# Local attention over a turn of four tiles: another order of steps in the four engine tables

## What is computed

```python
x = attn_layer(shift_tokens(x), Wqkv[i], q_scale[i], k_scale[i], Wo[i]) + x
x = ffn_layer(shift_tokens(x), ln_g[i], ln_b[i], W1[i], b1[i], W2[i], b2[i]) + x
# attn_layer: q, k, v = split(x @ Wqkv), 16 heads of 64
q = l2norm(q) * qs;  k = l2norm(k) * ksc          # then rotary embedding on both
sim = einsum('bhwie,bhwje->bhwij', bq, bk2) * 8   # windows of 32 see themselves and the one before
out = einsum('bhwij,bhwje->bhwie', softmax(masked sim), bv2) @ Wo
# ffn_layer: layernorm, then a * gelu(gate) @ W2
```

## Time and profile before

| | before |
|---|---|
| median of 3 runs | 2223.51 us (2223.18 to 2225.08) |
| profiled execution, whole time | 2226.05 us |
| its span, first to last instruction | 2224.2 us |
| busy in the span: PE, DVE, ACT, POOL | 88%, 66%, 63%, 63% |
| mean granted TensorE clock in the span | 0.909 |
| 24 `back` steps, first to last | 228.0 to 1794.3 us |

### The profile page before, as it was taken

How to read it: one execution, slowest core, us unless ns; L and a number is a source line. 1 busy time by engine, 2 the same in 40 slices (tenths; PEclk the granted TensorE clock), 3 DMA queues, 4 the chain that set the end, 5 groups by cost and what they waited for, 6 DMA issues and landing times. The chain is left out here.

```text
span 2224.2 us, 76642 instructions
## 1 busy us (share of the span) xinstructions
PE 1968.2 (88%) x31783; PEld 1328.2 (60%) x31783; DVE 1461.0 (66%) x2646; ACT 1401.0 (63%) x2766; POOL 1411.5 (63%) x1800
## 2 busy tenths in 40 slices
PE   5659999999999999999999999999999967887293
PEld 4526666666666666666666666666666645554262
DVE  2367777777778778787776877777877635333421
ACT  1167787677776777777777777777777722332041
POOL 1167888778887788887788877888778610001302
PEclk9779999999999999999999999999999966555596
DMA  2011111112110021101201112111101100001311
GB/s 90 0 25 38 61 45 29 38 29 75 32 38 29 29 82 32 31 28 38 76 29 31 29 38 76 28 31 32 34 29 29 31 7 0 1 0 32 99 40 47
DMA packets 55114, 82.88 MB, mean 37 GB/s; under 512 B 13140, under 2 KB 40042, under 8 KB 54002
## 3 DMA queue, kind: packets, MB, share of 16 engines
q1 hardware_dynamic: 53746, 75.88, 11.5%
q0 software_dynamic: 1024, 2.10, 0.3%
HBM read 25.66 MB, written 5.11 MB: 14 GB/s over the span
## 5 line engine op out<-in xcount | busy, mean ns | idle before, releaser
L1068 PE MATMUL b_bank_proj<-layer_weights,b_stream_t 128*128 128x512 f32 x1152 | 588.5, 612 | 34.2 <-DVE b_plain_moved L942 18.1
L942 DVE TENSOR_TENSOR b_plain_moved<-b_bank_proj,b_rope 128x1024 f32<-128x1024 f32 x384 | 463.9, 1219 | 189.0 <-ACT b_squares L828 137.1
L753 POOL TENSOR_TENSOR b_rotated<-b_plain_moved 128x1024 f32<-128x1024 f32 x192 | 453.8, 2363 | 23.6 <-DVE b_plain_moved L942 18.6
L768 POOL TENSOR_TENSOR b_rotated<-b_rotated,b_inv_norm 128x1024 f32<-128x1024 f32 x192 | 365.3, 1903 | 15.6
L859 ACT ACTIVATE b_k_t<-b_bank_shared 64x512 f32<-64x512 f32 x384 | 226.5, 590 | 125.9 <-PE b_bank_shared L1076 123.5
L828 ACT ACTIVATE b_squares<-b_bank_proj 128x512 f32<-128x512 f32 x384 | 229.3, 597 | 115.6 <-PE b_bank_proj L1068 111.2
L1068 PEld LDWEIGHTS b_bank_proj<-layer_weights,b_stream_t 128*128 128x128 f32 x1152 | 186.1, 191 | 135.9 <-issue 44.9
L773 POOL TENSOR_TENSOR b_probs<-b_probs,b_inv_sum 128x512 f32<-128x512 f32 x192 | 200.5, 1045 | 87.2 <-DVE b_inv_sum L963 85.8
L1076 PE MATMUL b_bank_shared<-const_tables,b_rotated 128*128 128x128 f32 x1536 | 233.2, 277 | 22.0 <-POOL b_rotated L768 21.9
L850 ACT ACTIVATE b_q_t<-b_bank_shared 64x512 f32<-64x512 f32 x384 | 225.6, 588 | 34.3 <-PE b_bank_shared L1076 31.5
L1076 PEld LDWEIGHTS b_bank_shared<-const_tables,b_rotated 128*128 128x128 f32 x1536 | 178.1, 141 | 113.4 <-issue 99.2
(11 more groups left out here) (319 smaller groups left out, 2929.1 us busy)
## 6 DMA issues: line engine op xcount, KB each, us to landing
b_v_shifted<-b_v SPq DMA_DIRECT2D x96, 384.0 KB, 3.5
layer_weights<-L_ffn_Wqkv SPq DMA_DIRECT2D x6, 1536.0 KB
b_v_shifted<-b_v SPq DMA_DIRECT2D x72, 128.0 KB, 3.4
d_w<-L_ffn_w SPq DMA_DIRECT2D x16, 256.0 KB, 5.6
layer_weights<-L_ffn_Wo SPq DMA_DIRECT2D x6, 512.0 KB
layer_weights<-L_ffn_W SPq DMA_DIRECT2D x6, 341.0 KB
sorted_rows<-d_zero SPq DMA_DIRECT2D x1, 1472.0 KB, 7.6
expert_rows<-d_sorted_out SPq DMA_DIRECT2D x23, 64.0 KB, 1.5
```

What stands on the lines that cost most here:

```text
L753: nc.gpsimd.tensor_tensor(out=turned[:, k, :], in0=pm[:, k, 0, :], in1=pm[:, k, 1, :], op=ALU.add).then_inc(add_done, 1)
L768: nc.gpsimd.tensor_tensor(out=tk, in0=tk, in1=repeat_last(rn[:, k, :], DH), op=ALU.mult).then_inc(rope_done, 1)
L942: nc.vector.tensor_tensor(to, src.to_broadcast(shape), tab.to_broadcast(shape), ALU.mult).then_inc(mul_done, 1)
L1068: nc.tensor.matmul(out, xs[:, b, t * P:(t + 1) * P], w, start=True, stop=True).then_inc(proj_full, 1)
```

## The change

Only the four lists change. Each holds the same steps as before, so every instruction is still there; their order, and with it the pipelining, differs. What the prediction speaks of, cut from the diff:

```diff
 POOL_TURN
-    ("add", -2, 1), ("clamp", -2, 1), ("weigh", -4, 1), ("rstd", -2, 0), ("rope", -2, 1), ("clamp", -1, 0),
-    ("weigh", -3, 0), ("add", -1, 0), ("weigh", -3, 1), ("clamp", -1, 1), ("rope", -1, 0), ("add", -1, 1),
-    ("rope", -1, 1), ("clamp", 0, 0), ("weigh", -2, 0), ("add", 0, 0), ("rope", 0, 0), ("weigh", -2, 1),
...
+    ("add", -1, 0), ("clamp", -1, 0), ("weigh", -3, 0), ("add", -1, 1), ("clamp", -1, 1), ("weigh", -3, 1),
+    ("rope", -1, 0), ("clamp", 0, 0), ("rope", -1, 1), ("weigh", -2, 0), ("add", 0, 0), ("weigh", -2, 1),
...
+    ("clamp", 2, 0), ("add", 2, 0), ("weigh", 0, 0), ("rope", 2, 0), ("clamp", 2, 1), ("weigh", 0, 1),
+    ("add", 2, 1), ("rope", 2, 1), ("rstd", -1, 0),
 DVE_TURN
-    ("norms", 5, 1), ("residual", 2, 0), ("soft", 4, 0), ("mul", 6, 0), ("norms", 6, 0), ("mul", 6, 1),
-    ("share", 4, 0), ("mul", 6, 2), ("soft", 4, 1), ("residual", 3, 0), ("mul", 6, 3), ("norms", 6, 1),
-    ("share", 4, 1), ("stats", 0, 0), ("soft", 5, 0), ("mul", 7, 0), ("norms", 7, 0), ("share", 5, 0),
+    ("share", 3, 1), ("down", -1, 0), ("mul", 5, 2), ("mul", 5, 3), ("norms", 5, 1), ("residual", 2, 0),
+    ("soft", 4, 0), ("mul", 6, 0), ("mul", 6, 1), ("norms", 6, 0), ("soft", 4, 1), ("share", 4, 0), ("mul", 6, 2),
+    ("residual", 3, 0), ("mul", 6, 3), ("norms", 6, 1), ("share", 4, 1), ("soft", 5, 0), ("mul", 7, 0),
 PE_TURN
-    ("project", 2, 1), ("pv", -1, 0), ("heads_t", 1, 0), ("project", 2, 2), ("heads_t", 1, 1), ("scores", 0, 1),
...
-    ("heads_t", 2, 0), ("project", 3, 1), ("probs_t", 0, 1), ("scores", 1, 1), ("project", 3, 2), ("pv", 0, 0),
-    ("heads_t", 2, 1), ("norm_t", -1, 0), ("project", 3, 3), ("heads_t", 2, 2), ("up", -1, 0), ("heads_t", 2, 3),
-    ("out", 0, 0), ("up", -1, 1), ("enter", 1, 0), ("probs_t", 1, 0), ("scores", 2, 0), ("up", -1, 2),
-    ("up", -1, 3), ("project", 3, 4), ("probs_t", 1, 1), ("project", 3, 5), ("heads_t", 3, 0), ("project", 4, 0),
-    ("project", 4, 1), ("pv", 1, 0), ("heads_t", 3, 1), ("project", 4, 2), ("scores", 2, 1), ("out", 1, 0),
...
+    ("scores", 0, 1), ("leave", -2, 0), ("heads_t", 1, 1), ("project", 2, 3), ("out", -1, 0), ("heads_t", 1, 2),
+    ("heads_t", 1, 3), ("project", 2, 4), ("back", -1, 0), ("probs_t", 0, 0), ("project", 2, 5), ("scores", 1, 0),
+    ("project", 3, 0), ("heads_t", 2, 0), ("project", 3, 1), ("probs_t", 0, 1), ("scores", 1, 1),
+    ("project", 3, 2), ("heads_t", 2, 1), ("pv", 0, 0), ("heads_t", 2, 2), ("heads_t", 2, 3), ("project", 3, 3),
+    ("norm_t", -1, 0), ("out", 0, 0), ("enter", 1, 0), ("up", -1, 0), ("scores", 2, 0), ("probs_t", 1, 0),
+    ("up", -1, 1), ("up", -1, 2), ("up", -1, 3), ("project", 3, 4), ("probs_t", 1, 1), ("project", 3, 5),
+    ("project", 4, 0), ("heads_t", 3, 0), ("project", 4, 1), ("heads_t", 3, 1), ("pv", 1, 0), ("scores", 2, 1),
+    ("project", 4, 2), ("out", 1, 0), ("heads_t", 3, 2), ("heads_t", 3, 3), ("up", -1, 4), ("up", -1, 5),
+    ("probs_t", 2, 0), ("scores", 3, 0), ("project", 4, 3), ("scores", 3, 1), ("probs_t", 2, 1),
 ACT_TURN
-    ("probs_t", -1, 0), ("probs_t", -1, 1), ("project", 2, 0), ("project", 2, 1), ("root", 1, 1), ("exp", 0, 0),
...
-    ("heads_t", 2, 3), ("gelu", -1, 0), ("probs_t", 1, 0), ("gelu", -1, 1), ("enter", 1, 0), ("gelu", -1, 2),
+    ("probs_t", -1, 1), ("project", 2, 0), ("exp", 0, 0), ("root", 1, 1), ("project", 2, 1), ("attended", -1, 0),
...
+    ("attended", 0, 1), ("project", 3, 3), ("heads_t", 2, 2), ("heads_t", 2, 3), ("root", 3, 0), ("gelu", -1, 0),
+    ("gelu", -1, 1), ("gelu", -1, 2), ("enter", 1, 0), ("root", 3, 1), ("project", 3, 4), ("project", 3, 5),
```

More of the change, by code:

```diff
@@ L498 @@
[L498 to L500 removed]
+    ("project", 0, 4), ("project", 0, 5), ("heads_t", 0, 0), ("heads_t", 0, 1), ("project", 1, 0),
+    ("project", 1, 1), ("pv", -2, 0), ("down", -2, 0), ("project", 1, 2), ("project", 1, 3), ("probs_t", -1, 0),
@@ L514 @@
[L514 to L518, removed]
+    ("root", 1, 0), ("probs_t", -1, 0), ("heads_t", 0, 3), ("project", 1, 4), ("project", 1, 5),
@@ new lines @@
+    ("probs_t", -1, 1), ("project", 2, 0), ("exp", 0, 0), ("root", 1, 1), ("project", 2, 1), ("attended", -1, 0),
+    ("heads_t", 1, 0), ("attended", -1, 1), ("project", 2, 2), ("root", 2, 0), ("leave", -2, 0), ("project", 2, 3),
+    ("exp", 0, 1), ("heads_t", 1, 1), ("heads_t", 1, 2), ("heads_t", 1, 3), ("project", 2, 4), ("project", 2, 5),
+    ("root", 2, 1), ("back", -1, 0), ("project", 3, 0), ("heads_t", 2, 0), ("project", 3, 1), ("probs_t", 0, 0),
+    ("probs_t", 0, 1), ("exp", 1, 0), ("project", 3, 2), ("heads_t", 2, 1), ("exp", 1, 1), ("attended", 0, 0),
@@ L519 @@
+    ("project", 4, 4), ("project", 4, 5), ("exp", 3, 1), ("heads_t", 4, 0), ("root", 4, 1), ("project", 5, 0),
+    ("project", 5, 1), ("heads_t", 4, 1), ("attended", 2, 0), ("project", 5, 2), ("attended", 2, 1),
+    ("project", 5, 3), ("heads_t", 4, 2),
 ]
 DVE_TURN = [
-    ("residual", 0, 0), ("hidden", -1, 0), ("mul", 4, 0), ("norms", 4, 0), ("share", 2, 0), ("mul", 4, 1),
-    ("mul", 4, 2), ("soft", 2, 1), ("hidden", -1, 1), ("hidden", -1, 2), ("residual", 1, 0), ("share", 2, 1),
-    ("mul", 4, 3), ("norms", 4, 1), ("soft", 3, 0), ("soft", 3, 1), ("share", 3, 0), ("mul", 5, 0),
@@ L531 @@
-    ("soft", 6, 0),
+    ("residual", 0, 0), ("mul", 4, 0), ("norms", 4, 0), ("mul", 4, 1), ("share", 2, 0), ("soft", 2, 1),
+    ("mul", 4, 2), ("share", 2, 1), ("residual", 1, 0), ("hidden", -1, 1), ("hidden", -1, 2), ("soft", 3, 0),
+    ("mul", 4, 3), ("soft", 3, 1), ("norms", 4, 1), ("share", 3, 0), ("mul", 5, 0), ("mul", 5, 1), ("norms", 5, 0),
+    ("share", 3, 1), ("down", -1, 0), ("mul", 5, 2), ("mul", 5, 3), ("norms", 5, 1), ("residual", 2, 0),
+    ("soft", 4, 0), ("mul", 6, 0), ("mul", 6, 1), ("norms", 6, 0), ("soft", 4, 1), ("share", 4, 0), ("mul", 6, 2),
@@ L532 @@
+    ("residual", 3, 0), ("mul", 6, 3), ("norms", 6, 1), ("share", 4, 1), ("soft", 5, 0), ("mul", 7, 0),
+    ("stats", 0, 0), ("norms", 7, 0), ("soft", 5, 1), ("mul", 7, 1), ("mul", 7, 2), ("share", 5, 0),
+    ("scale", 0, 0), ("mul", 7, 3), ("norms", 7, 1), ("share", 5, 1), ("hidden", 0, 0), ("soft", 6, 0),
 ]
 POOL_TURN = [
-    ("add", -2, 1), ("clamp", -2, 1), ("weigh", -4, 1), ("rstd", -2, 0), ("rope", -2, 1), ("clamp", -1, 0),
-    ("weigh", -3, 0), ("add", -1, 0), ("weigh", -3, 1), ("clamp", -1, 1), ("rope", -1, 0), ("add", -1, 1),
@@ L542 @@
+    ("rope", 0, 0), ("clamp", 0, 1), ("add", 0, 1), ("weigh", -1, 0), ("rope", 0, 1), ("clamp", 1, 0),
+    ("weigh", -1, 1), ("add", 1, 0), ("rope", 1, 0), ("clamp", 1, 1), ("add", 1, 1), ("rope", 1, 1),
+    ("clamp", 2, 0), ("add", 2, 0), ("weigh", 0, 0), ("rope", 2, 0), ("clamp", 2, 1), ("weigh", 0, 1),
+    ("add", 2, 1), ("rope", 2, 1), ("rstd", -1, 0),
 ]
```

22 lines of the change are left out of this document (5 added, 17 removed).

## The result

The changed kernel takes 2247.34 us (median of 4 runs, 2242.76 to 2250.38) against 2223.35 us of the kernel before on the same chip: 1.0106 times, with a 95% interval of 1.0083 to 1.0128. It is 1.1% slower, and above the range of the prediction. Its profiled execution took 2250.05 us, with a span of 2248.2, so 24.0 us more than before.

What follows compares the result with a forecast made beforehand. PE's own list was taken as the bound. From the profiled 2226.05 us, less 15 (layer starts), 0 (ordinary turns), plus 22 (clock), gave 2233, and 2.5 less on the median's scale 2230 us; range 2204 to 2241.

Steps and rivals of the forecast that it cites:

- PE's list: PE's work in an ordinary turn without waits: 65.1 us before the change, 65.0 after.
- The wait before norm_t: With rstd behind rope(2,1), the wait of heads_t(2,2) goes and PE waits 1.9 us before norm_t, bounds 1.2 to 2.1.
- The run saved: 11 runs of products on parts of the array for 12: 0.15 us saved a turn, bounds 0 to 0.19.
- Layer starts: A layer's first turn costs 1.0 us extra for 4.05: 3.0 us won, five times, 15 us; bounds 8 to 19.
- The clock: The wait before norm_t drops PE's clock to half in 14 of 23 turns, about 1.6 us each: 22 us lost.
- The feed of instructions: pv(1) and scores(2,1) as one run ask for 384 instructions in 3.03 us: 0.4 us a turn, bounds 0 to 1.
- Rival 2: Layer starts gain less, or feeding pv(1) with scores(2,1) costs 1 us a turn, no clock loss: 2222 us, no change; chance 0.14.
- The sign: Whole kernel against the one before: faster 0.37, same 0.20, slower 0.43; faster is below 2219 us, slower above 2228.
- rival 1: The wait before norm_t stays too short to cost the clock; only the layers' 15 us remain: 2208 us, faster; chance 0.34.
- The ordinary turn: Turns other than a layer's first: 67.45 us against 67.3 before, nothing won or lost; bounds 66.7 to 68.2.
- Rival 3: POOL becomes the bound, waiting at clamps for norms and pushing a rope into PE's way: 2240 us, slower; chance 0.06.

Runs made afterwards that it cites:

- e7: The changed kernel with a second power operation (1.04 us) added in GpSimd's normalisation, lengthening the idle before norm_t; 2294.8 us.
- e8: The kernel before with 320 waits on an already reached semaphore added on TensorE at the start of the fill, nothing else; 2245.0 us.

## Why the prediction was wrong, step by step

- **PE's list**: right. 65.1 and 65.0 us forecast, 65.10 and 64.96 measured.
- **The wait before norm_t**: right. 1.9 us forecast; the start is 1.90 us late in an ordinary turn, 1.74 of it idle, released by POOL as said, and the wait of heads_t(2,2) is gone. In PE's 17.85 us two slips nearly cancel: seven projections are 6.0 us at 0.86 each and not 6.3, and the group of `back`, 0.44, is not counted.
- **The run saved**: right, 0.14 to 0.15 us a turn. The Trainium skill, TensorEngine Tiling (Array Packing), Key Properties, let me fear a drain at pv before scores; the trace shows no cost of one (1.04 us from pv's second half to scores, 1.03 from scores to what follows).
- **Layer starts**: the size was right. The turns with a table took 68.65 to 70.30 us, within 0 to 1.5 of their neighbours; 1.0 was forecast. PE had no wait for the table any more; timelines of POOL and of DVE:
```profile
943.25 2.79 POOL L739 TENSOR_TENSOR b_rope<-const_tables,b_qk_scale 128x256 f32<-128x256 f32 x4
```
```profile
946.07 1.22 DVE L941 TENSOR_TENSOR b_plain_moved<-b_bank_proj,b_rope 128x1024 f32<-128x1024 f32 x1 [2.64 <-POOL b_rope L739]
```
DVE stands 2.64 us for it where it stood 7.21.
- **The clock**: failed. 14 falls at 1.6 us, 22 us, were forecast, and none came in these waits. I had put the point at about 1.3 us of idle, from one stop of 1.33 in the fill. At this wait, none of 22 idle times of up to 1.95 us was followed by a fall, and 16 of 22 of 2.37 us or more were (e7).
- **The feed of instructions**: failed, and this decided. I took 0.4 us a turn with bounds of 0 to 1 for pv(1) and scores(2,1) as one run. Measured in turns 1 to 21: 15.5 us at scores(2,1), 10.3 at scores(3,1), which I had not looked at, and 5.4 in pv(2) (each time from start to start, over what the step takes undisturbed): 31 us, 1.5 a turn, where the same places had 6.7 before. The step's fault was to read a gap as bad luck of one long product. It comes at an edge that can be counted, wherever PE gets there too soon after the fetch began, and the change brought dense steps together in two places. Rival 2 had named 1 us a turn for this feed, with a chance of 0.14: at its place, scores(2,1), it was 0.7, and the rest came at two places that it did not name.
- **The sign** came out as slower for the most part of another reason. Without the clock's 22 us my sum was 2208, rival 1; with the measured feed in place of 0.4 us in each of 23 turns it is 2233 (the 1.5 a turn of the three places) to 2239 (all 40.3 us of stops). The measured 2247 lies 8 us above that, and which term they belong to is not shown; turn 22, which I counted with the drain as unchanged, has 5.4 us more. So the way that it moved was forecast by luck: the 22 us that made the sum slower never came, and the stops at the edges that I had put at 9 us came to 31 to 40.
- **The ordinary turn**: 67.45 with bounds up to 68.2; measured 68.3 to 69.8 in turns 3 to 19, but for 70.99 in turn 4, which has a stretch at half clock. The mark I had set myself for a wrong forecast, a clock of 1.00 in ordinary turns, is what the windows show.
- Rival 2 came about in part, as said above, though the time did change. Rival 3 did not come about: POOL has the waits for the clamp (3.99 us for DVE at turn 8), but no rope was late for it.

Open is why 1.74 us before norm_t never lost the clock, while it fell behind 1.51 us in pv in e8, behind 1.33 in the fill, and in the kernel after behind 0.95 us in pv (turn 4) and 1.78 and 1.28 us in scores (turns 20 and 21), but not behind 1.36 and 1.24 us in scores (turns 15 and 18). The length of the idle alone does not sort these cases, and no run here told apart what does.
